# Causal mask of a transposed score tile: zeroed by GpSimd after the exponential, in place of a TensorE mask product, with a half's diagonal keys first

## The reference, cut to what matters

```python
qkv = hidden_states @ Wqkv                      # 32 query heads of 16, one key head, one value head
scores = einsum('bqhd,bkd->bhqk', q, k) * scale
causal = pos_k <= pos_q
scores = where(causal, scores + slope_h * (pos_k - pos_q), -1e30)
probs = softmax(scores)
attn = einsum('bhqk,bkd->bqhd', probs, v)       # then @ Wo
```

## Time and profile before

| | us |
|---|---|
| median of 3 runs (1262.68 to 1267.5) | 1265.94 |
| the profiled execution: its own time | 1263.67 |
| the profiled execution: span of the core | 1261.9 |
| first exponential of the second pass starts | 58.6 |
| last pv of the attention stage ends | 689.7 |

### The profile page before, as it was taken

One profiled execution on the slowest core, in us unless ns is written; L12 is line 12 of the kernel. 1 busy time (PEld: TensorE's weight loads), 2 busy tenths in 40 slices (PEclk: granted clock), 3 DMA queues, 4 the chain that ended last, 5 costly groups with the idle time before them and its releaser, 6 DMA issues.

```text
span 1261.9 us, 16721 instructions
## 1 busy us (share of the span) xinstructions
PE 1166.2 (92%) x6153; PEld 715.2 (57%) x6224; DVE 715.8 (57%) x1370; ACT 580.1 (46%) x1043; POOL 337.9 (27%) x365
## 2 busy tenths in 40 slices
PE   4779999999989999999999799999999999999995
PEld 4535533543443343344544567788788787766663
DVE  4468588678759898788832554251141142365553
ACT  5515456475727677884666334311111111234443
POOL 1214113211311060231013555311121111234554
PEclk9989999999999999999999999999999999999998
DMA  4451412410040311302320121230020132000304
GB/s 156 99 87 52 84 36 43 88 39 18 14 85 21 93 35 17 77 17 60 52 85 34 51 67 53 101 100 1 1 101 1 15 134 67 1 34 21 113 0 133
DMA packets 71695, 72.15 MB, mean 57 GB/s; under 512 B 39954, under 2 KB 45354, under 8 KB 71596
## 3 DMA queue, kind: packets, MB, share of 16 engines
q1 hardware_dynamic: 67412, 60.35, 19.2%
q0 software_dynamic: 3152, 8.63, 2.0%
q10 hardware_dynamic: 1056, 2.16, 0.5%
HBM read 51.86 MB, written 18.87 MB: 56 GB/s over the span
## 4 chain that ended last, share of the span: by engine, by line
PE 71%; issue 9%; DVE 7%; POOL 6%; ACT 3%; DMA 3%; SPq 1%; POOLq 0%; another core or an unknown queue 0%; DVEq 0%; ACTq 0%
PE PO L1407 10%; PE ST L1393 9%; PE bank L1314 9%; PE f_pair L56 6%; PE f_pair L58 6%; PE f_pair L57 6%; DVE mx L1125 3%; PE f_Y L1794 3%; PE f_Y L1796 3%; PE f_Y L1795 3%; PE ST L1395 2%; PE bank L1340 2%; PE bank L1317 2%; POOL l_rstd L1974 2%; PE bank L1342 2%
## 5 line engine op out<-in xcount | busy, mean ns | idle before, releaser
L1125 DVE TENSOR_REDUCE mx<-bank 128x1 f32<-128x512 f32 (+2 forms) x576 | 364.8, 684 | 99.8 <-PE bank L1317 55.2
L1048 ACT ACTIVATE PT<-ST 128x512 f32<-128x512 f32 x576 | 311.4, 600 | 106.9 <-PE ST L1393 62.5
L1314 PE MATMUL bank<-KS,QS 125*128 125x512 bf16 (+2 forms) x896 | 204.7, 309 | 13.5 <-DMA QS<-q_scratch 5.0
L1393 PE MATMUL ST<-QS,KS 128*128 128x512 bf16 x527 | 185.1, 383 | 9.0 <-DMA QS<-mparts 3.3
L1407 PE MATMUL PO<-PT,V 128*32 128x512 f32 x1152 | 152.8, 604 | 1.4 <-ACT PT L1048 1.0
L1314 PEld LDWEIGHTS bank<-KS,QS 125*128 125x128 bf16 x896 | 78.8, 99 | 114.3 <-DVE mx L1125 33.6
L56 PE MATMUL f_pair<-f_xT,gw 128*128 128x512 f32 (+1 forms) x352 | 140.0, 398 | 0.0
L1720 DVE TENSOR_TENSOR f_h<-f_h,f_pair 128x512 f32<-128x512 f32 (+1 forms) x44 | 30.2, 687 | 191.0 <-ACT f_h L1665 191.0
L58 PE MATMUL f_pair<-f_xT,gw 128*128 128x512 f32 (+1 forms) x352 | 138.0, 392 | 0.0
L57 PE MATMUL f_pair<-f_xT,gw 128*128 128x512 f32 (+1 forms) x352 | 137.8, 392 | 0.0
L1665 ACT ACTIVATE f_h<-f_pair 128x512 f32<-128x512 f32 (+1 forms) x44 | 26.3, 598 | 216.7 <-PE f_pair L58 216.7
(11 more groups left out here) (203 smaller groups left out, 1799.0 us busy)
## 6 DMA issues: line engine op xcount, KB each, us to landing
QS<-q_scratch SPq DMA_DIRECT2D x96, 128.0 KB
l_x<-x_dram SPq DMA_DIRECT2D x12, 512.0 KB, 4.2
q_scratch<-QP SPq DMA_DIRECT2D x36, 128.0 KB, 1.9
xres<-_attn_hidden_states_dram POOLq DMA_DIRECT2D x16, 256.0 KB, 3.0
x_dram<-xout POOLq DMA_DIRECT2D x16, 256.0 KB, 2.4
xin<-x_dram SPq DMA_DIRECT2D x4, 1024.0 KB, 7.7
f_xsum<-x_dram SPq DMA_DIRECT2D x4, 1024.0 KB, 7.1
x_dram<-f_xsum SPq DMA_DIRECT2D x4, 1024.0 KB, 4.6
```

The lines of the kernel that those rows point to most:

```text
L1048: act.activation(PT[:, quad % PT_RING, n % 4, :], ST[:, n % ST_RING, :], ACT.Exp).then_inc(p_done, 1)
L1125: v.tensor_reduce(mx[:, i % 2, z, h:h + m], at(u).rearrange("p (m k) -> p m k", m=m), AX.X, ALU.max).then_inc(bank_free_dve, 1)
L1314: last = pe.matmul(at(u)[:, j * w:(j + 1) * w], QS[0:ROWS1, slot, h + j, :], KS[b][0:ROWS1, k0:k0 + w], start=(j == 0 or not diag), stop=( ...
L1393: last = pe.matmul(dst, KS[b][0:ROWS2, kb * P:(kb + 1) * P], QS[0:ROWS2, slot, h:h + 4, :], start=True, stop=not diag)
```

## The change

Six things differ:

- The mask product of the second pass (L1395) is gone, and the second half of the mask table with it. The first pass keeps its masks.
- GpSimd gets a job "cut" for each of the 128 diagonal tiles: after ACT has written the tile's exponentials to `PT` it waits for `p_done`, and one `affine_select` in place over 128 x 512 fp32 sets those with key > query to zero. It raises `p_cut`.
- Every exponential gets a bias of -60 from a constant tile, so that unmasked scores above the row maximum don't overflow; the factor cancels in the division.
- A half's diagonal quad is its first and no longer its last: place 0 is the diagonal key block, place p is key block p - 1. Its pv waits for `p_cut`, those of the other quads for `p_done` as before. A score tile waits for its `ST` bank by `p_done`, so not for a cut.
- The planner drops 216 ns from a diagonal tile, knows a cut as 650 ns on GpSimd and prefers it (-1) where two jobs could start at the same time. The whole order of all engines is planned anew.
- In the planner SP's job "mdma" is put in the queue when mt3 is done, and no longer together with the transpose "mt". At "mt" the stack of block i + 2 is put in the queue if its slot is free, so it may now stand ahead of the maxima of block i.

```diff
 def diagonal(q):
-    i, _, kb = quad_place(q)
-    return kb == BLOCKS[i][1]
+    return quad_place(q)[2] == 0
+
+def key_block(q):
+    i, _, place = quad_place(q)
+    return place - 1 if place else BLOCKS[i][1]
+
+def cut_before(q):
+    i, a, _ = quad_place(q)
+    return 4 * (2 * i + a + 1)
...
-        if kind == "tile" and diagonal(u[1] // 4):
-            ms += 216
...
             if kind == "mt":
-                sp_issue(("mdma", u[1]), e + 2300)
                 if u[1] + AHEAD < NB:
                     stacks_due.append(u[1] + AHEAD)
         try_stacks()
...
-                out.append((max(t, free[e]), 1 if j[0] in ("exp", "stats") + TABLE_STEPS else 0, k, j))
+                out.append((max(t, free[e]), 1 if j[0] in ("exp", "stats") + TABLE_STEPS else -1 if j[0] == "cut" else 0, k, j))
...
             if kind == "exp":
-                end["exp", j[1]] = f + reads["act"]
+                end["read", j[1]] = f + reads["act"]
+                if diagonal(j[1] // 4):
+                    pend["pool"].append((("cut", j[1]), f + 100))
+                else:
+                    end["exp", j[1]] = f + reads["act"]
...
+            elif kind == "mt3":
+                sp_issue(("mdma", j[1]), done)
...
-            f = t + {"rstd": 1000, "norm": 8400, "fin": 5300, "clear": 5000, "fetch": 14000, "q3": 1400, "dl": 1700}[kind]
+            f = t + {"rstd": 1000, "norm": 8400, "fin": 5300, "clear": 5000, "fetch": 14000, "q3": 1400, "dl": 1700, "cut": 650}[kind]
...
+                elif kind == "cut":
+                    quad = i // 4
+                    pool.wait_ge(p_done, i + 1)
+                    at = PT[:, quad % PT_RING, i % 4, :].rearrange("p (m k) -> p m k", k=P)
+                    pool.affine_select(at, at, [[0, 4], [1, P]], ALU.is_ge, zero, base=0, channel_multiplier=-1).then_inc(p_cut, 1)
...
-                act.activation(PT[:, quad % PT_RING, n % 4, :], ST[:, n % ST_RING, :], ACT.Exp).then_inc(p_done, 1)
+                act.activation(PT[:, quad % PT_RING, n % 4, :], ST[:, n % ST_RING, :], ACT.Exp, bias=lowered[:, 0:1]).then_inc(p_done, 1)
...
-                dst, diag = ST[:, n % ST_RING, :], kb == BLOCKS[i][1]
-                last = pe.matmul(dst, KS[b][0:ROWS2, kb * P:(kb + 1) * P], QS[0:ROWS2, slot, h:h + 4, :], start=True, stop=not diag)
-                if diag:
-                    last = pe.matmul(dst, identb[:, :], mask[:, 1, :], start=False, stop=True)
-                last.then_inc(st_full, 1)
+                kb = key_block(n // 4)
+                pe.matmul(ST[:, n % ST_RING, :], KS[b][0:ROWS2, kb * P:(kb + 1) * P], QS[0:ROWS2, slot, h:h + 4, :], start=True, stop=True).then_inc(st_full, 1)
...
-                pe.wait_ge(p_done, 4 * q + 4)
-                if kb == 0:
+                if place == 0:
+                    pe.wait_ge(p_cut, cut_before(q))
+                else:
+                    pe.wait_ge(p_done, 4 * q + 4)
+                if place == 0:
                     pe.wait_ge(v_ready, keys_piece(i) + 1)
                     if 2 * i + a:
                         pe.wait_ge(ot_done, 2 * i + a)
```

More of the change, by code:

```diff
@@ L40 @@
 ROWS2 = P
+LOWERED = -60.0
 QSLOTS = 4
@@ L297, in pe_choices @@
             i = BLOCK_OF[n // 4]
-            t = known(("max", i), *([("exp", n - ST_RING)] if n >= ST_RING else []))
+            t = known(("max", i), *([("read", n - ST_RING)] if n >= ST_RING else []))
             out.append((t, act_load, ("tile", n)))
@@ L509, in commit @@
         elif e == "pool":
-            f = t + {"rstd": 1000, "norm": 8400, "fin": 5300, "clear": 5000, "fetch": 14000, "q3": 1400, "dl": 1700}[kind]
+            f = t + {"rstd": 1000, "norm": 8400, "fin": 5300, "clear": 5000, "fetch": 14000, "q3": 1400, "dl": 1700, "cut": 650}[kind]
             if kind == "fin":
                 end["fin", j[1]] = f + 100
+            elif kind == "cut":
+                end["exp", j[1]] = f + reads["pool"]
             elif kind in ("q3", "dl"):
@@ L686, in attention @@
         kvf = kvf2[:, 0, :]
-        mask = sb("mask", [P, 2, 512], BF16)
+        mask = sb("mask", [P, 512], BF16)
         gmask = sb("gmask", [P, 3])
+        lowered = sb("lowered", [P, 1])
         wo_s = [sb(f"wo{i}", [P, DC, D]) for i in range(2)]
@@ L758, in attention @@
         p_done = sem("p_done")
+        p_cut = sem("p_cut")
         pv_done = sem("pv_done")
@@ L888, in gpsimd @@
             pool.memset(half_neg[:, :], -0.5).then_inc(init, 1)
-            pool.wait_ge(init, 1)
+            pool.memset(lowered[:, :], LOWERED).then_inc(init, 1)
+            pool.wait_ge(init, 2)
             def piece_rstd(k):
@@ L942, in fetch_tables @@
                     pool.dma_start(dq.zpacked[g0:g0 + g, 0:w // PACK], mats[m][2]).then_inc(z_in, 16)
+            zero = pool.to_reg(0.0)
             piece_rstd(0)
@@ L977, in zero_slot @@
                 act.activation(QS[:, slot, :, :], half_neg[:, 0:1].unsqueeze(2).to_broadcast([P, NH, P]), ACT.Copy, scale=0.0).then_inc(qs_zero_act, 1)
-            act.wait_ge(init, 1)
+            act.wait_ge(init, 2)
             zero_slot(1)
@@ L1317, in row_max @@
                     last = pe.matmul(at(u).rearrange("p (m k) -> p m k", m=m)[:, :, w - P:w], identb[:, :],
-                                     mask[:, 0, 0:m * P].rearrange("p (m k) -> p m k", m=m), start=False, stop=True, skip_group_check=True)
+                                     mask[:, 0:m * P].rearrange("p (m k) -> p m k", m=m), start=False, stop=True, skip_group_check=True)
                 last.then_inc(bank_full, 1)
@@ L1385, in scores @@
             def scores(n):
-                i, a, kb = quad_place(n // 4)
+                i, a, _ = quad_place(n // 4)
                 b, slot, h = BLOCKS[i][0], i % QSLOTS, 16 * a + 4 * (n % 4)
@@ L1391, in scores @@
                     pe.wait_ge(p_done, n - ST_RING + 1)
-                dst, diag = ST[:, n % ST_RING, :], kb == BLOCKS[i][1]
-                last = pe.matmul(dst, KS[b][0:ROWS2, kb * P:(kb + 1) * P], QS[0:ROWS2, slot, h:h + 4, :], start=True, stop=not diag)
-                if diag:
-                    last = pe.matmul(dst, identb[:, :], mask[:, 1, :], start=False, stop=True)
-                last.then_inc(st_full, 1)
+                kb = key_block(n // 4)
+                pe.matmul(ST[:, n % ST_RING, :], KS[b][0:ROWS2, kb * P:(kb + 1) * P], QS[0:ROWS2, slot, h:h + 4, :], start=True, stop=True).then_inc(st_full, 1)
             def values(q):
-                i, a, kb = quad_place(q)
+                i, a, place = quad_place(q)
                 b, qb = BLOCKS[i]
-                pe.wait_ge(p_done, 4 * q + 4)
-                if kb == 0:
+                if place == 0:
[3 more added lines that the diff above has]
+                if place == 0:
                     pe.wait_ge(v_ready, keys_piece(i) + 1)
@@ L1406, in values @@
                 for j in range(4):
-                    last = pe.matmul(PO[32 * j:32 * (j + 1), :], V[b][:, kb, :], PT[:, q % PT_RING, j, :], start=(kb == 0), stop=(kb == qb))
+                    last = pe.matmul(PO[32 * j:32 * (j + 1), :], V[b][:, key_block(q), :], PT[:, q % PT_RING, j, :], start=(place == 0), stop=(place == qb))
                 last.then_inc(pv_done, 1)
@@ L2342, in shape_constants @@
         "c_identb": np.eye(P, dtype=np.float32).astype(bf),
-        "c_mask": np.stack([np.tile(mask, (1, 4)), np.tile(mask.T, (1, 4))], 1).astype(bf),
+        "c_mask": np.tile(mask, (1, 4)).astype(bf),
         "c_pos": pos.astype(bf),
```

## The result

| | before | changed | ratio, 95% interval |
|---|---|---|---|
| median of four runs each, us | 1265.26 | 1247.03 | 0.9855 [0.9834, 0.9877] |
| profiled execution, us | 1263.67 | 1246.18 | |
| span of its core, us | 1261.9 | 1244.4 | |

The change takes 18.2 us, where 14 was forecast: 1247 for 1252 us, inside the range and inside the forecast's own. Here is the page of the changed kernel, busy time and the two groups that matter; the columns are as in the earlier trace rows.

The account below looks back on a forecast made before the run. PE (TensorE, 92% busy) was taken to bound the kernel, with DVE close behind. Window gains of 0.9, 6.9, 3.0 and 2.0 us plus 1 for stacks made 13.8, say 14 us: median 1252 us, range 1238 to 1270.

Parts of the forecast that it names:

- The price of the removal: Second-pass mask products on PE: 128 at 0.215 us, 27.5 us in all, of which 21.0 us reach the end.
- the shares: Part of removed products' time reaching the end, by attention window: 75%, 75%, 60%, 100%; PE's 137 us of waits lengthen.
- The cut: GpSimd's affine_select on each of 128 diagonal tiles: 0.65 us each, 83 us in all, hidden in the mean.
- The lower and the upper rows: Bounds for one GpSimd cut: 0.57 us from memsets, 2.07 us from the operation with one input and two scalars.
- Where the cut is late: First pv of a half waiting for GpSimd: 0.85 us at uncovered small halves, plus collisions with norm, clear, fetch and fin.
- clear and fetch: GpSimd jobs from 448.64 to 464.76, 16.1 us, holding up cuts behind them; 1.5 us charged in the third window.
- SP's reorder: Stack transfers in SP's queue start nearly a block earlier and don't meet the maxima: 1 us gained.
- (a): Rival, chance 0.22: all 27.5 us of removed mask products reach the end, collisions fall elsewhere: 1238 us.
- (b): Rival, chance 0.18: DVE or ACT sets the pace, handovers show at about half the halves, 1 or 2 us left: 1264.
- (c): Rival, chance 0.07: GpSimd's cut costs 1.27 to 1.5 us, like an operation with two inputs: 1258 to 1265 us.
- (d): Rival, chance 0.06: GpSimd's cut costs 2.07 us, like the one-input operation; 21 us slower, 1287 us.
- (e): Rival, chance 0.05: stacks get ahead of wanted maxima in SP's queue at 7 of 14 blocks, costing 20 us: 1272 us.

Follow-up runs that it names:

- order held: Kernel before without the second pass's mask products, 60 added to the maxima, planner still counting their 216 ns so every engine's order stays: 1245.47 us, ratio 0.9847.

## Why the prediction was right

**The price of the removal: right in all, not by stage.** 27.5 us of products, 21.0 expected at the end, 19 measured with the order unchanged. One profile each shows where it was gained, by the time at which ACT copies a half's `PO` (L1061, L1089):

| us gained up to | forecast, products | measured, order held | forecast, change | measured, change |
|---|---|---|---|---|
| half 4 copied (106.8 before) | 2.6 | 0.6 | 0.9 | 2.4 |
| half 16 copied (429.7) | 10.5 | 10.0 | 7.8 | 8.5 |
| half 25 copied (644.9) | 15.0 | 14.4 | 10.8 | 19.9 |
| first product with `f_xT` (703.0) | 21.0 | 18.0 | 12.8 and 1 for stacks | 17.5 |

With the order held the first stage gave 0.6 for 2.6, and the last, where I had every product counting, 3.6 for 6.0; the second gave 9.4 for 7.9. In the change the third stage gave 11.4 for the 3.0 of my sum, and from there to the end 2.4 us were lost where I had 2.0 gained. So the total is better than its parts. The reason that I gave for the shares, waits that grow where a product goes, isn't borne out either: they grew by 3 us with the order held.

**The cut: right.** 0.65 us taken, 0.638 measured, and the waits of the pv on GpSimd are 6.5 us of weight loads and 3.1 us of products, under the 10 I gave. The lower and the upper rows were not near; the planner's own figure, held against its neighbours, was.

**Where the cut is late: the size isn't settled.** I charged 8 us, and the runs give about 4, between 0 and 8. The handover from ACT to GpSimd, taken as 0.1 us, is 0.07 where GpSimd stood waiting. The 1.5 us for clear and fetch were not paid in this run, since the cuts of that half were just through:

```profile
447.67 2.41 POOL L984 TENSOR_SCALAR_AFFINE_SELECT PT<-PT 128x512 f32<-128x512 f32 x4 [8.94 <-ACT PT L1076]
450.03 0.23 POOL L951 MEMSET f_h<- 18x172 int32 x1
...
465.69 0.51 POOL L964 DMA_DIRECT2D f_h<-n_L_ffn_down_qzeros_dram  x1
470.68 1.22 POOL L984 TENSOR_SCALAR_AFFINE_SELECT PT<-PT 128x512 f32<-128x512 f32 x2 [4.48 <-ACT PT L1076]
```

The next half's cuts come 4.5 us after the last of the issues. The fin in the last block stood ahead of the cuts as forecast, but I had said there was no more work to cover it, and there was: the output products shown above. Two smaller slips stand in this part. Three quads at the mean of 4.4 us are 13 us, and not 9 to 12. And clear and fetch, planned at 5.0 + 14.0 = 19.0 us, took 16.1, so not every plan of that table is close.

**SP's reorder: mis-sized.** 1 us taken, 4 us measured alone (interval 1.8 to 6.5 us).

**The bias: a price left out.** I wrote that no instruction is added and charged nothing. It adds about 90 ns to each of 576 instructions. That cost 2.4 us in the old order and nothing measurable in the new. The trace of before held the hint, and I didn't read it. Two of its groups by shape, an activation with two pointers and one with none:

```profile
L2094 ACT ACTIVATE l_xn<-l_x,l_shift,l_rstd 128x512 f32<-128x512 f32 x36 | 27.3, 806 | 40.9 <-POOL l_shift L1976 40.9
...
L1061 ACT ACTIVATE OT<-PO 128x512 f32<-128x512 f32 x32 | 19.2, 598 | 33.0 <-PE PO L1407 33.0
```

**Missing from the sum: the plan.** Every edit that the planner sees makes a new order for all engines. The runs put that at 8 us between two orders for the same work, and at 15 us for the diagonal-first order with the masks kept. The change's order happened to carry the diagonal quad in front without such a loss: 15 us for products and SP, 4 lost to cuts, and 18 measured, so about 7 us (up to 11, if the cuts cost 8) came from the order with the diagonal first. (The 7 us are a difference of ratios whose intervals are some 3 us each way; that the order as such does it, and not one lucky plan, isn't shown.) The forecast came out close partly by luck, because these errors cancel: 8 us lost and about 7 won by orders that the sum didn't have, 3 more from SP, and by the middle value 4 more from cover.

**The rivals.** (a), all 27.5 us, fell: even with the order fixed it is 19. (b) had its sign, the three waits grown by nearly what the masks took (22 us), without its result. The sign doesn't follow the time: the waits are 141 us with the order held, 162 in the run without masks planned anew, and 150 and 159 in the changed kernel without and with the pointer, which are equally fast. Yet in the run without masks planned anew 60% of the products' time was eaten. (c) and (d) fell with the cut's 0.638 us, but their sums were wrong where it counts. I worked them out from GpSimd's load in a window and had the sign turn at 1.5 us. Between 0.64 (18 us faster) and 1.29 us (36 us slower) a straight line turns at 0.86. The failed step is "in large halves PE has p1 banks and further tiles for that time": it has them only where the plan put them ahead of the pv, and for a later cut it had not. The forecast didn't depend on it, as its cut was as long as the plan had it. With the plan told, my 21 us stood against 29. (e) is not seen: score tiles wait less for maxima, 2.2 and 1.9 us.

## What to carry to other kernels

With a fixed order on each engine, the cover of a moved operation is what was placed ahead of its reader, sized by the planned cost: 0.65 us planned and done cost about 4 us, 1.29 us done under the same plan cost 54 more. Measure the operation first and put that number in the plan. And when an edit also makes the order new, run it once with the order held: here 19 us became 11 by nothing but the plan.

## What the runs showed of the hardware

An affine_select of 128 x 512 fp32 in place takes GpSimd 0.638 us (0.625 to 0.658 over 128), half of its two-input tensor_tensor (1.27) and less than a third of its tensor_scalar with two pointers (2.07): one input doesn't by itself make it slow. A pointer bias lengthens an exponential of that size by 92 ns, 600 to 692; in a row they start every 0.57 us, for 0.49 without it. And in the run with three affine_selects, where PE stood still so often, the mean granted clock was 0.938, for 0.986 in the changed kernel, and 0.76 for 0.92 between 57 and 120 us. A product of the pv took 675 ns in the mean for 606. PE's busy time grew by 43 us for the same products; how much of that is the clock, and how much products that no longer overlap, wasn't told apart.
